# Decoder layer: pair 4 mixed alone, gate ahead of the factor, ScalarE and TensorE in the closing norm

## Chip, cores and metric

One core of one Trainium2 chip. The metric is the device time of one execution in microseconds; a kernel's time is the median of its runs. Engines: TensorE (PE), VectorE (DVE), ScalarE (ACT), GpSimd (POOL) and SyncE (SP, which here only issues transfers).

## What is computed

One decoder layer in float32 on x of 16 x 56 x 128, with post-norm after each of three blocks.

```python
def layernorm(x): return (x - mean(x)) / sqrt(var(x) + 1e-5)

# block 1: gated mixer
z = causal_conv4(x @ in_proj_w) + conv_b         # values, gate, scores
p_w = exp(clip(score_scale * s_raw)) * time_weight
re, im = cumsum(p_w * poly * cos(x_val * theta)) / den, cumsum(... sin ...) / den
rs = rsqrt(mean(re**2 + im**2) + 1e-5)           # the factor, per head
y = re * rs * norm_scale @ W_re + im * rs * norm_scale @ W_im
x = layernorm(x + (y * silu(gate)) @ out_proj_w)
# block 2: attention over a context of 1500 x 96
q, k, v = x @ Wq + bq, ctx @ Wk + bk, ctx @ Wv + bv
x = layernorm(x + softmax(q @ k.T / sqrt(128)) @ v)
# block 3: 8 experts, top 2 of them per token, then two norms
h = relu(x @ W1[e].T + b1[e]); o = h @ W2[e].T + b2[e]
x = layernorm(layernorm_gamma_beta(x + sum(router_w[e] * o)))
```

## The kernel before, in words

Each engine has its own hand-written list of instructions, in strict order, and meets the others through counting semaphores: an instruction that waits holds all that stand behind it on its engine. The 896 tokens are eight pairs of batch rows (112 tokens, 0 to 7), and for block 1 two halves of four pairs (c = 0, 1).

**Block 1** works with channels on partitions. For each half: projection and convolution (L490), angles, products, scans (L1242), group sums and squares (L500, L509). Then VectorE makes the variance (`variance`, L1281), ScalarE turns it into the factor (`factor`, L887 and L889), VectorE multiplies factor and gate and then y (`gated`, L1288 and L1291), TensorE projects out (`project_out`, L518), and VectorE adds x (`mixed`, L1297), takes the moments (`mixed_stats`, L1304, L1307) and, after ScalarE's reciprocal deviation (`mix_inv_std`), normalises (`mixed_norm`, L1313). `X1_PARTS` says which pairs are normalised, turned (`turn_x1`, L526; `x1T_copy`, L905) and made into queries (`query_keys`, L533; `queried_keys`, L917) together: pair 0, pairs 1 to 3, and pairs 4 to 7. `keep_warm` (L478) are matmuls on constants.

**Block 2** is a loop of seven turns and a last one. In turn i TensorE makes the scores of pair i+1 (L543), sums the context of pair i-1 (L566), turns the weights of pair i (L553, in three thirds), and finishes pair i-1 (`turn_sum`, `values`). VectorE takes the maximum (L1366) of pair i+1, copies turned weights (L1470) and makes the norm of pair i-1 (L1477 to L1489); ScalarE makes the exponential (L926). The second half of block 1 is woven into turns 0 to 2. Also woven in: the router (logits, top two, ranks, slots), the split of the expert weights into a high and a low float16 half (high on ScalarE, `split_high`, L991 and L993; low on POOL for experts 0 to 4, `split_low`, L1734; m_wh and m_wl count them in order of (weight, expert)), and of x2 into row halves (`high_rows`, L981; `low_rows`, L1725). POOL's list then goes on: after the low halves of (0,4) and (1,4) it makes the low rows of pair 4 and then scatters the rows of pairs 2 to 6 to the experts' slots in memory, two scatters a pair (L1750), with short pauses between.

**Block 3.** SP waits for all 14 scatters and loads the first tile of each expert (L453). TensorE runs the sequence: pair 7 with experts 0 to 4, 20 tiles of 128 rows (each turned, L744; hidden layer, L765 and L767; output, L784), pair 7 with experts 5 to 7. ScalarE weights a tile's output (L1097), and POOL scatters it to `ret` (L1832).

**Tail.** SP loads `ret` for pairs 0 to 6 in four parts (L464). TensorE adds both returned rows to x2 in PSUM (L806). q = 0 to 3 are two pairs each; pair 7 is summed in `acc` by VectorE and is in q = 3. On VectorE, `returned(q)` takes the moments (L1668, L1671), and `last_sum(q)` centres and multiplies by gamma (L1679), multiplies by the reciprocal deviation and adds x2 + beta (L1684), and takes the second moments (L1688, L1691). ScalarE makes the reciprocal deviations (`final_inv_std`, L893 and L895) and the last norm (`final_norm`, L1123), for which VectorE prepares the bias (`final_bias`, L1698). SP stores two pairs at a time (L468).

The functions, with their lines:

## Time and profile before

| | |
|---|---|
| median of 3 runs | 206.45 us (205.98 to 206.97) |
| the profiled execution, its own time | 205.7 us |
| its span | 203.9 us |
| busy: PE, DVE, ACT, POOL | 173.8, 154.4, 117.6, 61.7 us |
| granted TensorE clock, mean | 0.97 |

The span is what the profiler recorded, from the first to the last event; the 1.8 us beside it belong to the execution's own time. All times below count from the span's start. In a timeline row stand the start, the duration, engine, line, operation and operands, how many instructions were merged, and in brackets how long the engine was idle before and what released it. Starts of neighbouring instructions can lie closer than their durations, as they overlap by a few tens of ns.

### The profile page before, as it was taken

Reading aid. Unit: us, or ns where it says so; the run is one execution under the profiler, and the core shown is the slowest. Engines: PE = TensorE matmul, PEld = TensorE weight load, DVE = VectorE, ACT = ScalarE, POOL = GpSimd, SP = SyncE. Lnnn points to the kernel's source line nnn. Section 1 sums busy time; section 2 is a strip of 40 time slices with the busy share of each in tenths; the row PEclk is TensorE's granted clock in tenths of the full one; section 3 lists DMA queues with packets and bytes.
Section 4 is the critical chain, followed back from the end, with each engine's and each line's share of the span. In section 5 each row is a group of like instructions: output and inputs, shape, how many; then the busy total and the mean of one; then the engine's idle time right before and its main releaser. Section 6 shows DMA issues by size and latency. Waiting matters only on the chain.

```text
span 203.9 us, 4768 instructions
## 1 busy us (share of the span) xinstructions
PE 173.8 (85%) x1721; PEld 127.5 (63%) x1721; DVE 154.4 (76%) x394; ACT 117.6 (58%) x246; POOL 61.7 (30%) x82
## 2 busy tenths in 40 slices
PE   7999999969799978799799998785999999996400
PEld 6554556644353664564656787584999999994300
DVE  1659999988979668558967885677688888743890
ACT  2189979722664515697676954442566777650544
POOL 4000000000040000029697568881045655550000
PEclk9999999999999999999999999997899999999965
DMA  6999999993899278779856911104234100005011
GB/s 133 335 212 294 229 296 259 407 412 140 217 351 323 81 253 208 270 187 309 208 200 189 345 47 36 35 25 106 57 83 104 40 22 26 19 0 161 2 45 45
DMA packets 13467, 34.20 MB, mean 168 GB/s; under 512 B 2096, under 2 KB 5606, under 8 KB 13443
## 3 DMA queue, kind: packets, MB, share of 16 engines
q1 hardware_dynamic: 12356, 32.27, 53.0%
q0 software_dynamic: 1088, 1.62, 2.6%
q8 instruction: 14, 0.23, 0.5%
q14 instruction: 9, 0.07, 0.1%
HBM read 28.01 MB, written 6.38 MB: 169 GB/s over the span
## 4 chain that ended last, share of the span: by engine, by line
PE 53%; DVE 20%; issue 10%; POOL 8%; ACT 4%; DMA 2%; POOLq 0%; ACTq 0%; DVEq 0%; SPq 0%
PE bank L490 9%; POOL ret L1832 8%; PE bank L543 8%; PE bank L566 6%; PE bank L509 5%; PE bank L500 5%; PE bank L553 5%; PE bank L478 4%; DVE neg_max L1366 2%; PE bank L767 2%; PE bank L784 2%; DVE ph L1470 2%; DMA ctxT_slot<-ret 1%; DVE xtok L1684 1%; PE bank L806 1%
## 5 line engine op out<-in xcount | busy, mean ns | idle before, releaser
L1084 ACT ACTIVATE ctx_slot<-bank 128x512 f16<-128x512 f32 (+1 forms) x28 | 16.3, 582 | 18.8 <-PE bank L767 18.7
L1832 POOL DMA_INDIRECT ret<-ctx_slot,ctxT_slot x20 | 19.7, 986 | 24.5 <-ACT ctx_slot L1097 20.8
L1598 DVE SCALAR_TENSOR_TENSOR ctx_slot<-bank,ctx_slot 128x512 f16<-128x512 f32 (+1 forms) x28 | 18.8, 671 | 9.6 <-ACT ctx_slot L1084 7.2
L543 PE MATMUL bank<-ctxT_slot,w_conv 97*64 97x500 f32 x96 | 21.8, 589 | 2.4 <-ACT pc L926 1.4
L1754 POOL TENSOR_TENSOR home<-home 128x896 f32<-128x896 f32 x1 | 2.1, 2077 | 55.3 <-ACT home L882 55.3
L490 PE MATMUL bank<-xpad,w_conv 128*128 128x448 f32 x48 | 18.5, 544 | 0.0
L784 PE MATMUL bank<-home,ctx_slot 128*112 128x128 f16 (+1 forms) x192 | 14.7, 227 | 3.2 <-DVE ctx_slot L1598 3.2
L1366 DVE TENSOR_REDUCE neg_max<-bank 120x1 f32<-120x1500 f32 x8 | 13.7, 1714 | 4.5 <-PE bank L543 4.5
L1734 POOL TENSOR_TENSOR home<-w_raw,home 128x512 f16<-128x512 f32 x10 | 11.5, 1164 | 14.8 <-DVE neg_max L1366 14.8
L1242 DVE TENSOR_TENSOR_SCAN home<-reset,home 128x896 f32<-128x896 f32 x8 | 15.8, 2008 | 0.0
L566 PE MATMUL bank<-ctx_slot,ph 125*64 125x96 f32 x336 | 15.4, 248 | 0.0
L784 PEld LDWEIGHTS bank<-home,ctx_slot 128*112 128x112 f16 (+1 forms) x192 | 12.6, 121 | 3.7 <-DVE ctx_slot L1598 3.5
L490 PEld LDWEIGHTS bank<-xpad,w_conv 128*128 128x128 f32 x48 | 9.1, 193 | 9.2 <-issue 8.7
L1750 POOL DMA_INDIRECT slots<-mix,slot_i x14 | 13.5, 963 | 4.6 <-issue 3.7
L566 PEld LDWEIGHTS bank<-ctx_slot,ph 125*64 125x64 f32 x336 | 14.1, 133 | 1.2 <-issue 0.7
L478 PE MATMUL bank<-reset 128*128 128x224 f32 x48 | 13.4, 424 | 1.4 <-DVE reset L1145 1.4
L543 PEld LDWEIGHTS bank<-ctxT_slot,w_conv 97*64 97x64 f32 x96 | 6.2, 133 | 13.0 <-issue 10.9
L765 PE MATMUL bank<-half_sb,b_hl 128*128 128x112 f16 (+1 forms) x64 | 13.8, 221 | 0.3 <-DVE turned_late L1561 0.3
L500 PE MATMUL bank<-home,w_blk 128*128 128x448 f32 x32 | 12.9, 545 | 0.0
L478 PEld LDWEIGHTS bank<-reset 128*128 128x128 f32 x48 | 10.7, 235 | 2.9 <-DVE reset L1145 1.4
L893 ACT ACTIVATE lnv<-mv,cst 112x2 f32<-112x2 f32 (+3 forms) x11 | 3.2, 293 | 15.6 <-DVE mv L1307 6.3
L767 PE MATMUL bank<-ctx_slot 128*128 128x128 f16 x144 | 12.0, 219 | 0.0
(223 smaller groups left out, 433.5 us busy)
## 6 DMA issues: line engine op xcount, KB each, us to landing
ctx_slot<-ctx SPq DMA_DIRECT2D x16, 576.0 KB, 5.7
ctxT_slot<-ctx_T SPq DMA_DIRECT2D x16, 562.5 KB, 9.5
w_raw<-w SPq DMA_DIRECT2D x16, 256.0 KB, 6.9
slots<-w_raw SPq DMA_DIRECT2D x4, 910.0 KB, 26.1
ctxT_slot<-slots SPq DMA_DIRECT2D x20, 65.0 KB, 1.9
...
```

What stands on the lines that cost most here:

```text
L478: mm = pe.matmul(bank[:, to, 0:HW // 2], reset[:, 0:D], reset[:, 0:HW // 2], start=True, stop=True)
L490: mm = pe.matmul(bank[:, Z[c, g], 0:HW], w_conv[:, g, k, :], xpad[:, HB * c:HB * (c + 1), k:k + L], start=(k == 0), stop=(k == TAPS - 1))
L500: mm = pe.matmul(bank[:, Y_BANK[c], 0:HW], w_blk[:, j, :], terms[:, j * HW:(j + 1) * HW], start=(j == 0), stop=(j == 2 * M - 1))
L543: mm = pe.matmul(bank[j * GAP:j * GAP + rows, n, 0:SN], qk_all[:, at:at + rows], ctxT_slot[:, s, j, n * SN:(n + 1) * SN], start=True, stop ...
L566: mm = pe.matmul(bank[j * GAP:j * GAP + rows, SUM_BANKS[i], 0:DC], expT_sb[i][:, c, j * GAP:j * GAP + rows], ctx_slot[0:KP, s, j, c, :], s ...
L767: mm = pe.matmul(to, w[:, 0, part, at], x[:, half, 0:cols], start=False, stop=(m == 2))
L784: mm = pe.matmul(to, h_[:, n % 3, f, 0:cols], w[:, 1, part, f * D:(f + 1) * D], start=False, stop=(h_ is hl and f == FC - 1))
L1084: nc.scalar.activation(hh[:, n % 3, :, 0:cols], bank[:, n % 3, :].rearrange("p (f t) -> p f t", f=FC) [:, :, 0:cols], ACT.Relu).then_inc(t ...
L1242: return V.tensor_tensor_scan(sums[:, w], reset[:, 0:W2], terms[:, w], 0.0, ALU.mult, ALU.add)
L1366: V.tensor_reduce(neg_max[0:GT, :], bank[0:GT, 0:SB, 0:SN], AX.XY, ALU.max, negate=True).then_inc(a_max, 1)
L1598: V.scalar_tensor_tensor(hl[:, n % 3, :, 0:cols], bank[:, n % 3, :].rearrange("p (f t) -> p f t", f=FC) [:, :, 0:cols], 0.0, hh[:, n % 3, ...
L1832: G.indirect_dma_start(ret[:], bass.IndirectOffsetOnAxis(ap=xs_u[:, t, D + 1:D + 2], axis=0), out_st[:, t % OB, :], None, bounds_check=2 * ...
```

## The change

Block 1, second half: `X1_PARTS` has four parts, the third being pair 4 and the fourth pairs 5 to 7. Pair 4 is mixed, normalised in turn 1 and turned and queried in turn 2; pairs 5 to 7 are mixed in turn 1, have their moments and norm in turn 2 and are turned and queried in turn 3. y is multiplied by the gate before the factor is there, and by the factor afterwards (one multiply behind it, as before two); the projection of the second half moves ahead of the last third of the turned weights and its sum. In the front, the norm of pair 0 moves before the second half of the cosine products, and two of three `keep_warm` go. ScalarE's `split_high` are dealt out anew over the turns: 1, 2, 1, 3, 2 in turns 1 to 5 and one behind the loop (before: 1, 3, 2, 2, 2). POOL's list is the same.

Tail: pair 7 is done first and alone. For pairs 0 to 6 VectorE centres, ScalarE multiplies by the reciprocal deviation (`scaled`), TensorE adds that and x2 + beta in PSUM (`with_x2`), and VectorE takes the second moments there. The last norm is ScalarE's for q = 0 and 1, and VectorE's for pair 7, q = 2 and pair 6. There are five stores instead of four.

```diff
-X1_PARTS = (range(0, 1), range(1, PPH), range(PPH, PAIRS))
-T_BANK, QK_BANK = (4, 3, 7), (6, 5, 7)
+X1_PARTS = (range(0, 1), range(1, PPH), range(PPH, PPH + 1), range(PPH + 1, PAIRS))
+T_BANK, QK_BANK = (4, 3, 7, 7), (6, 5, 7, 7)
...
+SUM_AT, NORM_AT = (3, 7, 0, 1), (2, 5, 6, 4)
...
-    for q in range(4):
-        sp_.wait_ge(f_out, q + 1)
-        w = slice(2 * q, 2 * q + 2)
+    for n, w in enumerate((slice(XP, PAIRS), slice(0, 2), slice(2, 4), slice(4, 6), slice(6, XP))):
+        if n in (1, 2):
+            sp_.wait_ge(f_out, n)
+        else:
+            sp_.wait_ge(f_outv, n - 1 if n else 1)
         sp_.dma_start(out[:, w, :], x1[:, w, :]).then_inc(s_store, 16)
-    sp_.wait_ge(s_store, 16 * 4)
...
     def turn_x1(n):
         pe.wait_ge(s_x1, n + 1)
+        if n == 3:
+            pe.wait_ge(a_qksb, n)
...
-        pe.wait_ge(a_qksb, 1 if i == 0 else 2 if i < PPH else 3)
+        pe.wait_ge(a_qksb, 1 if i == 0 else 2 if i < PPH else 3 if i == PPH else 4)
...
     def logits(i):
         pe.wait_ge(a_x2T, i + 2)
+        if i == 0:
+            pe.wait_ge(a_qksb, 4)
...
         if i in (4, 6):
             ranks((4, 6).index(i))
+        if i in (2, 3):
+            turn_x1(i)
         if i:
             context_sum(i - 1)
         if i == 2:
-            turn_x1(2)
+            query_keys(2)
         turn_weights(i, 0)
         turn_weights(i, 1)
-        if i == 2:
-            query_keys(2)
+        if i == 1:
+            project_out(1)
+        if i == 3:
+            query_keys(3)
         if i:
             turn_sum(i - 1)
         turn_weights(i, 2)
         if i == 0:
             group_sums(1, 1)
-        if i == 1:
-            project_out(1)
         if i:
             values(i - 1)
...
-    keep_warm(3, 0)
+    keep_warm(1, 0)
...
+    def added(to, rows_, start=False, stop=False):
+        width = rows_.shape[1] * D
+        return pe.matmul(bank[0:PT, to, 0:width], ident[0:PT, 0:PT], rows_, start=start, stop=stop)
+
+    def returns(q):
+        w = slice(2 * q, min(2 * q + 2, XP))
+        added(SUM_AT[q], x2[:, w, :], start=True)
+        pe.wait_ge(g_ld[q], 16)
+        added(SUM_AT[q], got[:, w, 0, :])
+        added(SUM_AT[q], got[:, w, 1, :], stop=True).then_inc(f_y, 1)
+
+    def with_x2(q):
+        w = slice(2 * q, min(2 * q + 2, XP))
+        added(NORM_AT[q], x2b[:, w, :], start=True)
+        pe.wait_ge(f_scaled, q + 1)
+        added(NORM_AT[q], acc[:, w, :], stop=True).then_inc(f_sum, 1)
 
     pe.wait_ge(t_hl, len(SEQUENCE))
...
+    pe.wait_ge(t_acc, E)
+    pe.wait_ge(m_x2b, PAIRS)
+    returns(0)
+    returns(1)
+    returns(2)
+    with_x2(0)
+    returns(3)
+    with_x2(1)
+    with_x2(2)
+    with_x2(3)
...
     def attend_turn(i):
+        if i in (2, 3):
+            x1T_copy(i)
         if i + 1 < PAIRS:
             weights_exp(i + 1)
         if i == 1:
             factor(1)
         if i == 2:
-            x1T_copy(2)
+            queried_keys(2)
+            mix_inv_std(3)
         if i:
             turned_sum(i - 1)
+        if i == 1:
+            mix_inv_std(2)
+        if i == 3:
+            queried_keys(3)
         turned_copy(i)
         if i == 0:
             square(1, M, M + 2)
             square(1, M + 2, 2 * M)
-        if i == 2:
-            queried_keys(2)
         if i:
-            if i == 1:
-                mix_inv_std(2)
             attended_inv_std(i - 1)
         if i == 1:
             split_high(0, 0)
         if i == 2:
             split_high(1, 0)
             split_high(0, 1)
-            split_high(1, 1)
         if i == 3:
             high_rows(0)
         if i >= 3:
             high_rows(i - 2)
-        if 3 <= i < 6:
-            split_high(0, i - 1)
-            split_high(1, i - 1)
         if i in (3, 5):
             route_weights((3, 5).index(i))
+        if i == 3:
+            split_high(1, 1)
+        if i == 4:
+            split_high(0, 2)
+            split_high(1, 2)
+            split_high(0, 3)
+        if i == 5:
+            split_high(1, 3)
+            split_high(0, 4)
...
     high_rows(PAIRS - 3)
+    split_high(1, POOL_SPLITS - 1)
     turned_copy(PAIRS - 1)
...
+    def scaled(q):
+        act.wait_ge(f_cent, q + 1)
+        act.wait_ge(f_rstd, q + 2)
+        for j in range(2 * q, min(2 * q + 2, XP)):
+            ins = nc.scalar.activation(acc[:, j, :], acc[:, j, :], ACT.Copy, scale=rstd[:, j:j + 1])
+        ins.then_inc(f_scaled, 1)
...
+            ins = nc.scalar.activation(x1[:, j, :], bank[0:PT, NORM_AT[q], (j % 2) * D:(j % 2 + 1) * D],
+                                       ACT.Identity, bias=nmr[:, j:j + 1], scale=rstd2[:, j:j + 1])
         ins.then_inc(f_out, 1)
...
     final_inv_std(0, False)
+    final_inv_std(0, True)
     final_inv_std(1, False)
-    final_inv_std(0, True)
+    scaled(0)
     final_inv_std(2, False)
-    final_norm(0)
+    scaled(1)
     final_inv_std(1, True)
     final_inv_std(3, False)
+    scaled(2)
+    final_norm(0)
+    final_inv_std(2, True)
+    final_inv_std(4, False)
+    scaled(3)
     final_norm(1)
-    final_inv_std(2, True)
-    final_norm(2)
     final_inv_std(3, True)
-    final_norm(3)
+    final_inv_std(4, True)
...
+    def with_gate(c):
+
+        dve.wait_ge(s_gate, c + 1)
+        dve.wait_ge(s_ys, c + 1)
+        return own.mark(V.tensor_tensor(y_gated[:, c, :], y_gated[:, c, :], gate[:, c, :], ALU.mult))
+
+    def gated(c, multiplied):
+
+        own.need(multiplied)
         dve.wait_ge(s_f, c + 1)
-        dve.wait_ge(s_gate, c + 1)
-        a = own.mark(V.tensor_tensor(gate[:, c, :], gate[:, c, :], sc[:, c, :], ALU.mult))
...
     variance(0)
-    weights(1)
-    gated(0)
+    multiplied = with_gate(0)
+    weights(1, between=lambda: gated(0, multiplied))
     cos_terms(1, 0)
     dve.wait_ge(s_xtok, 16)
-    summed = mixed(0)
+    summed = mixed(0, range(PPH))
     mixed_stats(0, summed)
+    mixed_stats(1, summed, between=lambda: mixed_norm(0))
     cos_terms(1, 1)
-    mixed_norm(0)
-    mixed_stats(1, summed)
...
         maximum(i + 1)
         if i == 1:
             dens.append(denominator(1, scan_weights()))
             variance(1)
+            multiplied = with_gate(1)
+        inverse(i)
+        if i == 1:
+            gated(1, multiplied)
         if i == 2:
-            mixed_norm(2)
-        inverse(i)
+            mixed_stats(3, last_mixed)
         if i >= 2:
             x2T_copy(i - 2)
         if i in (4, 6):
             place((4, 6).index(i))
         if i:
             sum_copy(i - 1)
-        if i == 1:
-            gated(1)
         turned_copy(i)
+        if i == 2:
+            mixed_norm(3)
         if i == 0:
             scan_im(1, 0)
             scan_im(1, 1)
             scan_y(1)
         if i == 1:
-            mixed_stats(2, mixed(1))
+            mixed_stats(2, mixed(1, X1_PARTS[2]))
+            last_mixed = mixed(1, X1_PARTS[3])
+            mixed_norm(2)
...
+    def last_pair():
+
+        j = XP
+        dve.wait_ge(t_acc, E)
+        dve.wait_ge(m_x2b, PAIRS)
+        moments(0, lambda j: acc[:, j, :], f_var)
+        dve.wait_ge(f_var, 1)
+        a = own.mark(V.scalar_tensor_tensor(acc[:, j, :], acc[:, j, :], mv[:, j, 0:1], par("gamma", PT),
+                                            ALU.subtract, ALU.mult))
+        own.need(a)
+        dve.wait_ge(f_rstd, 1)
+        a = own.mark(V.scalar_tensor_tensor(acc[:, j, :], acc[:, j, :], rstd[:, j:j + 1], x2b[:, j, :],
+                                            ALU.mult, ALU.add))
+        own.need(a)
+        moments(0, lambda j: acc[:, j, :], f_var2)
...
+        moments(q + 1, returned_at, f_var)
+        dve.wait_ge(f_var, q + 2)
+        for j in range(2 * q, min(2 * q + 2, XP)):
+            ins = V.scalar_tensor_tensor(acc[:, j, :], returned_at(j), mv[:, j, 0:1], par("gamma", PT),
+                                         ALU.subtract, ALU.mult)
+        ins.then_inc(f_cent, 1)
+
+    def summed(q):
+        dve.wait_ge(f_sum, q + 1)
+        moments(q + 1, normed_at, f_var2)
...
+    def vector_final(n):
+
+        dve.wait_ge(f_rstd2, n + 1)
+        for j in range(XP, PAIRS) if n == 0 else range(2 * n - 2, min(2 * n, XP)):
+            ins = V.tensor_scalar(x1[:, j, :], normed_at(j) if n else acc[:, j, :], mv[:, j, 0:1],
+                                  rstd2[:, j:j + 1], ALU.subtract, ALU.mult)
+        ins.then_inc(f_outv, 1)
+
...
+    last_pair()
     returned(0)
+    vector_final(0)
     returned(1)
-    last_sum(0)
+    summed(0)
     returned(2)
     final_bias(0)
-    last_sum(1)
+    summed(1)
     returned(3)
     final_bias(1)
-    last_sum(2)
-    last_sum(3)
-    final_bias(2)
-    final_bias(3)
+    summed(2)
+    summed(3)
+    vector_final(3)
+    vector_final(4)
```

## Rows read from the trace of the kernel before

**Rows 1.** Busy time in two windows: PE, PEld, DVE, ACT, POOL, granted clock, DMA.

```profile
141.00:144.00 3.00, 3.00 (x34) 3.00 (x33) 1.62 (x4) 1.04 (x2) 0.00 (x0) 0.50 0.52 116
...
193.70:198.80 5.10, 0.00 (x0) 0.00 (x0) 4.86 (x23) 2.28 (x9) 0.00 (x0) 0.64 0.15 45
```

**Rows 2.** Timeline of VectorE, starts of the maximum: start, duration.

```profile
51.08 1.72 DVE L1366 TENSOR_REDUCE neg_max<-bank 120x1 f32<-120x1500 f32 x1 [0.54 <-PE bank L543]
...
65.39 1.69 DVE L1366 TENSOR_REDUCE neg_max<-bank 120x1 f32<-120x1500 f32 x1
...
79.22 1.71 DVE L1366 TENSOR_REDUCE neg_max<-bank 120x1 f32<-120x1500 f32 x1
...
88.79 1.72 DVE L1366 TENSOR_REDUCE neg_max<-bank 120x1 f32<-120x1500 f32 x1 [1.74 <-PE bank L543]
...
96.86 1.71 DVE L1366 TENSOR_REDUCE neg_max<-bank 120x1 f32<-120x1500 f32 x1
```

**Rows 3.** Timeline of VectorE, gate, mix and norm of turns 1 and 2.

```profile
72.07 0.61 DVE L1288 TENSOR_TENSOR mix<-mix 128x448 f32<-128x448 f32 x1
...
75.57 0.69 DVE L1297 TENSOR_TENSOR x<-bank,xtok 112x512 f32<-112x512 f32 x1 [1.10 <-PE bank L518]
...
80.85 1.11 DVE L1313 TENSOR_SCALAR x<-x,mv,rstd 112x128 f32<-112x128 f32 x4
```

**Rows 4.** Timeline of TensorE, turns 1 and 2.

```profile
75.68 2.73 PE L543 MATMUL bank<-ctxT_slot,w_conv 97*64 97x500 f32 x12
...
82.02 0.60 PE L526 MATMUL bank<-small_sb,x 112*128 112x112 f32 x4 [0.22 <-DVE x L1313]
...
83.34 0.92 PE L533 MATMUL bank<-xv,w_qk 128*97 128x448 f32 x2
```

**Rows 5.** Timeline of ScalarE, a weight split and the loop's end.

```profile
78.83 0.61 ACT L991 ACTIVATE w_raw<-w_raw 128x512 f32<-128x512 f32 x1
79.47 0.63 ACT L993 ACTIVATE home<-w_raw 128x512 f16<-128x512 f32 x1
...
120.27 0.40 ACT L981 ACTIVATE mix<-rows_late 112x256 f16<-112x256 f32 x1
122.04 0.56 ACT L931 COPY home<-bank 125x480 f32<-125x480 f32 x1 [1.37 <-PE bank L553]
```

**Rows 6.** Timeline of POOL, around the first scatter of group 1.

```profile
115.73 2.28 POOL L1734 TENSOR_TENSOR home<-w_raw,home 128x512 f16<-128x512 f32 x2
119.69 0.68 POOL L1725 TENSOR_TENSOR mix<-rows_late,mix 112x256 f16<-112x256 f32 x1 [1.68 <-ACT mix L981]
120.52 0.95 POOL L1750 DMA_INDIRECT slots<-mix,slot_i  x1 [0.15 <-POOL mix L1725]
...
136.16 0.95 POOL L1750 DMA_INDIRECT slots<-mix,slot_i  x1 [0.17 <-issue]
```

**Rows 7.** SP's queue, landing of its line 453, and TensorE at tile 0.

```profile
138.50 3.65 SPq L453 DMA_DIRECT2D ctxT_slot<-slots  x8
...
DMA to landing us min/median/max: 1.8/2.3/3.0
...
140.54 0.68 PE L784 MATMUL bank<-home,ctx_slot 128*112 128x128 f16 x4 [2.41 <-DVE ctx_slot L1598]
141.01 0.42 PE L744 MATMUL bank<-half_sb,ctxT_slot 128*128 128x128 f16 x2
```

**Rows 8.** Groups by shape, 186 to 204 us: busy us, mean ns, idle before.

```profile
L1123 ACT ACTIVATE x<-xtok,nmr,rstd 112x128 f32<-112x128 f32 x8 | 3.5, 481 | 1.7 <-DVE nmr L1698 1.7
L806 PE MATMUL bank<-ctxT_slot,small_sb 112*112 112x256 f32 x12 | 3.2, 387 | 1.7 <-DMA ctxT_slot<-ret 1.7
...
L1684 DVE SCALAR_TENSOR_TENSOR xtok<-xtok,rstd,rows_late 112x128 f32<-112x128 f32 x8 | 2.5, 349 | 0.1
L893 ACT ACTIVATE lnv<-mv,cst 112x2 f32<-112x2 f32 x8 | 2.3, 293 | 9.3 <-DVE mv L1671 6.1 <-DVE mv L1691 3.0
```

**Rows 9.** Timeline, the last instruction of ScalarE.

```profile
200.75 0.88 ACT L1123 ACTIVATE x<-xtok,nmr,rstd 112x128 f32<-112x128 f32 x2 [0.23 <-DVE nmr L1698]
```

88 lines of the change are left out of this document (32 added, 56 removed).

## The prediction

> **What bounds the kernel now.** I read the page's strip of 40 slices first: TensorE is at nine tenths or more almost everywhere and breaks off only near slice 27 and at the end. The chain that ended last then shows four stretches in which different things are late.
>
> First, the attention turns. The starts of the maximum on VectorE mark them [rows 2]. From turn 4 on one turn takes some 7.5 to 8.7 us, but turn 1 (65.39 to 79.22) takes 13.8 and turn 2 (79.22 to 88.79) takes 9.6. In these two turns the second half of the first block (squares, gate, output projection, four pairs mixed, normalised and turned at once) stands in the engines' queues ahead of the attention's next scores, which TensorE could start only at 75.68 [rows 4].
>
> Second, the scatters on POOL. From the first one of group 1 at 120.52 ten scatters run to 137.1 with only POOL's own work between them (low halves, weights, pauses) [rows 6]; the one that began at 136.16 releases the loads of the tiles at 138.50 [rows 7].
>
> Third, the experts. TensorE turns tile 0 at 141.01 [rows 7]; the load, issued at 138.50, landed by the shortest and the median time of its line at 140.3 to 140.8. VectorE's table of tiles let TensorE go at 140.54 [rows 7], so both paths end within about 0.5 us of each other. From there to 184 TensorE is full, and that stretch of 43 us has a fixed length.
>
> Fourth, the tail. Between 193.7 and 198.8 VectorE is busy 4.86 of 5.1 us, ScalarE 2.28, TensorE nothing [rows 1]. VectorE bounds it, until the last ScalarE norm, which starts at 200.75 [rows 9] and ends at 201.63; span 203.9.
>
> **Front (before turn 0).** The gate multiply moves ahead of the factor's arrival and only one multiply stays behind it, so y_gated is ready 0.6 us sooner (one of two multiplies; the second half's takes 0.61 [rows 3]). The projection, the first transpose and the first scores follow it on TensorE, and the first maximum, which waited 0.54 us for these scores [rows 2], then comes when VectorE is free. I take -0.5 (ends 0 and -0.65). Two fewer warming groups cost nothing: TensorE waits for VectorE there anyway.
>
> **Turn 1.** The factor is covered by the gate multiply; one multiply remains, and the projection stands before the last third of the turned weights instead of behind it. Second gate ready: 71.75 instead of 73.34 (0.5 of it from the front). The copies of the turned weights start 1.2 us earlier, the scores of turn 2 at 74.2 instead of 75.68. Behind them VectorE no longer does four pairs at once: one pair mixed (0.3, from the 0.69 of four [rows 3]), its statistics, then the add of the other three (0.55) while ScalarE finds the first deviation. Its path to the attended norm is now 3.6 us from 73.25, done at 76.85, as TensorE's scores end (74.2 + 2.73 [rows 4]). Maximum of turn 2 at 77.0 instead of 79.22 [rows 2]: -2.2 so far.
>
> **Turn 2.** On TensorE one transpose (0.2) and a query of one pair (0.25) replace four transposes of 0.60 together and a query of 0.92 [rows 4]. Before, the transposes waited for VectorE's four norms (1.11 at 80.85 [rows 3]); now the norm of pair 4 was done in turn 1, and statistics (1.0) and norm (0.85) of pairs 5 to 7 lie beside TensorE's 7.8 us of work. Next maximum at 84.8 instead of 88.79: -4.0.
>
> **Turn 3.** What was put off is paid here: three transposes (0.5), a query of three pairs (0.75), and a wait of some 0.1 us, as the logits use its bank and the next scores need its copy. Turn 3 was VectorE-bound by 0.5 us at its end, which covers part. Next maximum 93.8 instead of 96.86 [rows 2]: -3.1.
>
> **Turns 4 to 6.** ScalarE now splits three weight halves in turn 4 instead of two; a split is 0.61 + 0.63 [rows 5]. It had 0.4 us of idle time, so the exponential is 0.8 us late, of which 0.3 to 0.45 reach TensorE through the turned sum. Against it TensorE waited 0.8 us in turn 4 behind VectorE, part of which goes. I take **g = 3.1 us** as the gain at the end of the loop (ends 2.0 and 3.9: all of turn 3 and the late exponential uncovered; or turn 4's wait gone as well).
>
> **The wait this adds, on POOL.** POOL's list is unchanged: low half of (0,4), of (1,4), low rows of pair 4, first scatter of group 1. The high half of (1,4) used to be made in turn 5; POOL had both low halves by 118.01 and then waited 1.68 us for the rows [rows 6]. Now it comes after ScalarE's rows of pair 5, which end at 120.67, in the 1.37 us hole before the turned copy at 122.04 [rows 5]. In the old clock: high half at 121.85, low half at 123.1 (1.14 each, half of 2.28 [rows 6]), scatter at 123.9 instead of 120.52. That is 3.4 us later; the loop brings it forward by g. Net for the scatter chain: 3.4 - 3.1 = +0.3. Queued behind it on POOL are all ten scatters, which nothing else paces, and behind these SP's loads. The load of tile 0 lands at 140.6 to 141.1 against 141.0 for TensorE's turn before, so **the loop's gain of 3.1 is almost all lost: 0.0** (with g at its ends: +1.3 and -0.7). TensorE arrives at tile 0 three microseconds early and stands.
>
> That gap touches the clock. After the present gap TensorE's granted clock was 0.50 for 141 to 144 [rows 1], that is 1.2 GHz, and full again behind it. It will stop sooner and resume as late, so the slow stretch ends somewhat later: +0.2 (ends 0 and +0.5). The Trainium skill ("TensorE: Matmul & The Clock Gate", HAM oscillation) says the same of idle gaps; the trace agrees with its half rate.
>
> **Tail.** (a) Pair 7 is done from 184.75, while VectorE waits for the returns until 187.7; of its work moments, centring and scaling, 1.2 us, leave the busy stretch. (b) Seven scale-and-adds, 0.349 each and paced 0.31 [rows 8], leave VectorE: 2.2. (c) Pair 7's final norm enters, +0.34, and 0.2 for small gaps that two pairs shared. VectorE's work from 187.65 to its last moments is then 11.45 - 1.2 - 2.2 + 0.34 + 0.2 = 8.6 us, which would end at 196.3. (d) The hand-overs: centred -> ScalarE scale (0.87 a pair, as two of the 0.481 norms [rows 8]) -> TensorE add (0.387 a 256-wide matmul [rows 8], twice that at the lower clock) -> moments. Written out in order, VectorE waits 0.35 at the first sum, 0.5 at the second bias and 0.5 at the last sum, since ScalarE has 9.0 us of work from 188.5 in strict order: last moments at 197.7. (e) Deviation 0.53 (0.293 [rows 8] and 0.20), and one norm of 0.34 on VectorE: 199.2. Before, 2.5 us lay behind the last moments (two ScalarE norm pairs). With issue and landing as before the end moves from 203.9 to 201.7: **-2.2**. Ends: no waits, -3.6; every one of seven hand-overs costing 0.3 more, and the fifth output transfer queued behind the fourth, -0.5. I take the middle since the rows of each part are in the same stretch.
>
> By row, ScalarE's 112x128 pass costs 0.481 and VectorE's scale-and-add 0.349 [rows 8]. The Trainium skill ("ScalarE: Activation LUTs", Rules for kernel authors) says to use VectorE, not ScalarE, for add and mul. By that rule alone the sum would gain nothing at (b); I go by the window, where VectorE is full and ScalarE less than half.
>
> **Sum.** 0.0 + 0.2 - 2.2 = -2.0 on the profiled execution, whose time is 205.7: 203.7. It lay 0.75 below the median of 206.45; the median becomes 204.4.
>
> **Rivals.**
> 1. *The loop's gain reaches the tiles.* If the last low half is ready earlier than I count, or scatters can close up, tile 0 comes up to 2.5 us sooner: 204.4 - 2.5 = 201.9. For: the table of tiles and all TensorE work arrive early. Against: POOL's strict order and its solid row of scatters [rows 6].
> 2. *ScalarE becomes the tail's bound.* Its 9.0 us in strict order, with the 0.481 passes ahead of deviations that VectorE awaits, could swallow the 2.2: 206.2 to 206.6. It decides if ScalarE idles under 0.3 us from 188.5 on. The skill's rule above would have this outcome. Against: ScalarE's 2.28 of 5.1 [rows 1].
> 3. *Slower: the wait on the last high half outweighs all.* If turns 1 and 2 give nothing (the same VectorE work in pieces ends as late), the front's 0.5 stays and turn 3's 1.35 us and the exponential's 0.45 are paid: g = -1.3. The scatters then start 4.7 late, the load of tile 0 lands near 145.25, +4.25; with +0.2 and the tail's -2.2 the time is 208.7. It decides from g = -0.1 down (3.5 - 0.45 of slack + 0.2 - 2.2 is +1). Against: the 13.8 us of turn 1 are plainly queueing.
> 4. *Small gains*: g = 2 and a tail of -1.2 give +1.3 + 0.2 - 1.2: 206.7.
>
> **Chances.** Forecast, 203.2 to 205.4: 0.56. Rival 1: 0.17. Rivals 2 and 4, no change: 0.20. Rival 3: 0.07. A run of this kernel can tell about 0.5% (1 us) from no change. Faster 0.73, same 0.20, slower 0.07. The range takes in the forecast, most of rival 1 and the better part of 2 and 4: 202.2 to 206.2.
>
> **What would show it.** Right: maxima near 77, 84.8 and 93.8; an idle time of POOL ahead of its low half of (1,4), with the first group-1 scatter at 120.5 to 121.2; TensorE idle 3 us or more before the turn of tile 0, released by a DMA, near 141; VectorE's last norm near 199.3. Wrong: scatter (2,0) before 119 (rival 1) or after 123.5 (rival 3); ScalarE without idle time in the tail (rival 2).

## The result, and the profile after

| | before | after |
|---|---|---|
| median of 17 runs each, same chips | 205.93 us (205.09 to 207.30) | 203.24 us (201.37 to 205.70) |
| ratio, 95% interval | | 0.9845 (0.9813 to 0.9876) |
| the profiled execution, its span | 205.7, 203.9 us | 202.66, 200.9 us |
| busy: PE, DVE, ACT, POOL | 173.8, 154.4, 117.6, 61.7 us | 178.9, 154.1, 119.0, 61.5 us |

Three of the 17 executions after (204.50, 204.56 and 205.70) lie over 1.5% above the fastest of their kernel, and such executions are left out of every ratio and interval and of the medians in the table of the experiments; without them the median after is 202.87 us (201.37 to 204.15). The kernel is 1.55% faster, 3.1 us by these medians, 2.7 by those of the table above and 3.0 by the two profiled executions. The forecast was 204.4 us, 1.0% under the median it started from (206.45, of three runs; with 17 that median is 205.93). The direction holds and 203.24 lies in the range, but the gain is half as large again as forecast.

**Loop.** Timeline of VectorE after, the maximum at the start of turn 1 and the last one (start, duration), answering to [rows 2]:

```profile
64.50 1.69 DVE L1421 TENSOR_REDUCE neg_max<-bank 120x1 f32<-120x1500 f32 x1
...
108.71 1.71 DVE L1421 TENSOR_REDUCE neg_max<-bank 120x1 f32<-120x1500 f32 x1
```

Those between start at 76.39, 84.10, 92.56 and 100.05. Turn 1 shrank from 13.83 to 11.89 us and turn 2 from 9.57 to 7.71; turn 3 took 8.46 instead of 8.07. Against before the loop is 4.30 us ahead at 92.56, 5.56 ahead at 100.05 (105.61), and only 4.33 ahead at 108.71 (113.04). Two small VectorE operations say where it was lost again (same view):

```profile
106.39 2.09 DVE L1544 TENSOR_SCALAR rows_late<-res,attend_mv,attend_rstd 112x128 f32<-112x128 f32 x1
...
110.78 2.21 DVE L1471 TENSOR_TENSOR slot_c<-chosen,slot_e 112x32 f32<-112x32 f32 x1
...
116.51 0.35 DVE L1544 TENSOR_SCALAR rows_late<-res,attend_mv,attend_rstd 112x128 f32<-112x128 f32 x1
```

The norm L1544 takes 0.35 us at 116.51 and 2.09 at 106.39. The third row is also the norm of pair 5, the last thing that POOL's rows need from the loop; before it stood at 119.34, so the loop's gain there is g = 2.83. These starts are of one profile each, and the front moves between profiles: the first maximum stands at 50.20 after and 51.08 before, but at 50.40 in the kernel "tail only" below, which has the old front.

**POOL.** Timeline of POOL after, answering to [rows 6]:

```profile
111.78 1.16 POOL L1813 TENSOR_TENSOR home<-w_raw,home 128x512 f16<-128x512 f32 x1
119.09 1.15 POOL L1813 TENSOR_TENSOR home<-w_raw,home 128x512 f16<-128x512 f32 x1 [6.16 <-ACT home L1020]
120.20 0.68 POOL L1804 TENSOR_TENSOR mix<-rows_late,mix 112x256 f16<-112x256 f32 x1
121.04 0.94 POOL L1829 DMA_INDIRECT slots<-mix,slot_i  x1 [0.15 <-POOL mix L1804]
...
136.67 0.95 POOL L1829 DMA_INDIRECT slots<-mix,slot_i  x1 [0.17 <-issue]
```

POOL stands 6.16 us for the high half of (1,4), which ScalarE makes behind the loop (L1020 at 118.39). The first scatter of group 1 is at 121.04 against 120.52, although the loop is almost three microseconds early; the last begins at 136.67 instead of 136.16, and SP's loads at 139.07 instead of 138.50 [rows 7].

**TensorE at tile 0.** Timeline of TensorE after, answering to [rows 7], and the windows around it (columns as in [rows 1]):

```profile
139.60 0.43 PE L795 MATMUL bank<-home,ctx_slot 128*112 128x128 f16 x4 [2.42 <-DVE ctx_slot L1659]
140.87 0.33 PE L755 MATMUL bank<-half_sb,ctxT_slot 128*128 128x128 f16 x2 [0.84 <-DMA ctxT_slot<-slots]
```

```profile
126.00:130.00 4.00, 3.26 (x26) 2.59 (x27) 1.63 (x11) 1.95 (x8) 3.26 (x6) 0.67 0.11 32
130.00:134.00 4.00, 4.00 (x45) 3.96 (x45) 1.85 (x10) 1.67 (x5) 3.25 (x6) 0.50 0.11 30
134.00:138.00 4.00, 3.13 (x54) 2.85 (x52) 3.62 (x14) 2.12 (x4) 3.25 (x7) 0.98 0.11 31
138.00:141.00 3.00, 0.56 (x7) 0.42 (x7) 2.33 (x8) 0.00 (x0) 0.80 (x3) 1.00 0.25 64
141.00:144.00 3.00, 3.00 (x33) 3.00 (x32) 1.16 (x4) 1.06 (x2) 0.00 (x0) 0.50 0.45 97
```

The first two of these windows before:

```profile
126.00:130.00 4.00, 2.62 (x17) 1.78 (x18) 3.23 (x19) 1.68 (x7) 3.24 (x8) 1.00 0.10 29
130.00:134.00 4.00, 3.65 (x62) 3.29 (x63) 2.32 (x14) 2.03 (x6) 3.25 (x7) 1.00 0.12 33
```

The turn begins at 140.87 instead of 141.01, released by the load. TensorE stands 2.42 us for VectorE's table of tiles, as it did before (2.41 [rows 7]), and 0.84 us more for the load; only these 0.84 are new. So the loop's gain is lost in two places. One is the load, which comes no earlier because the scatters do not. The other is TensorE itself. It begins pair 7's hidden layer at 128.11 instead of 130.94, the whole 2.83 us early, but the granted clock is down to 0.50 for 130 to 134, where it was 1.00 before. Its last work ahead of the table ends at 137.18 instead of 138.13, and the table lets it go at 139.60 instead of 140.54: 0.94 us early.

**Tail.** The first returned part reaches TensorE at 186.44 (186.54 before); the span ends 14.46 us later instead of 17.36. Timeline after, the end of VectorE's and ScalarE's work, answering to [rows 9]:

```profile
197.00 0.29 ACT L920 ACTIVATE lnv<-mv,cst 112x2 f32<-112x2 f32 x1
197.31 0.18 DVE L1724 BATCH_NORM_AGGREGATE mv<-stat 112x2 f32<-112x6 f32 x1
197.32 0.20 ACT L922 ACTIVATE rstd<-lnv 112x2 f32<-112x2 f32 x1
197.52 0.29 ACT L920 ACTIVATE lnv<-mv,cst 112x1 f32<-112x1 f32 x1
197.56 1.05 DVE L1773 TENSOR_SCALAR x<-bank,mv,rstd 112x128 f32<-112x128 f32 x3
197.85 0.20 ACT L922 ACTIVATE rstd<-lnv 112x1 f32<-112x1 f32 x1
```

The last moments end at 197.49 (199.15 before), and the last deviation (197.52 to 198.05) is made while VectorE already normalises pairs 4 and 5. The window 193 to 198 reads:

```profile
193.00:198.00 5.00, 1.61 (x8) 0.90 (x6) 3.57 (x19) 4.38 (x17) 0.00 (x0) 1.00 0.09 26
```

VectorE, 4.86 of 5.1 us before [rows 1], has 1.4 us of idle time; ScalarE is now the fuller one at 4.38. VectorE's longer waits are these three, at the first sum, the second bias and the last sum:

```profile
191.32 0.49 DVE L1721 BATCH_NORM_STATS2 stat<-bank 112x6 f32<-112x128 f32 x2 [0.72 <-PE bank L816]
...
195.53 0.16 DVE L1767 SCALAR_TENSOR_TENSOR nmr<-mv,rstd 112x2 f32<-112x2 f32 x1 [0.59 <-ACT rstd L922]
...
196.97 0.30 DVE L1721 BATCH_NORM_STATS2 stat<-bank 112x6 f32<-112x128 f32 x1 [0.60 <-PE bank L816]
```

None of this is what one would see if VectorE's work alone set the new end.

### The profile page after: what moved, and what is told of

It reads as the page before. It is cut to its first block, busy times and chain, and to the rows that moved or that the text cites. A ratio compares the mean times of both kernels' runs of the same rounds, so it can differ in the third digit from the quotient of the medians.

```text
span 200.9 us, 4804 instructions
## 1 busy us (share of the span) xinstructions
PE 178.9 (89%) x1735; PEld 131.3 (65%) x1735; DVE 154.1 (77%) x390; ACT 119.0 (59%) x257; POOL 61.5 (31%) x82
## 3 DMA queue, kind: packets, MB, share of 16 engines
q0 software_dynamic: 1088, 1.62, 2.6%
## 4 chain that ended last, share of the span: by engine, by line
PE 25%; POOL 21%; issue 17%; ACT 5%; DVE 5%; DMA 4%; POOLq 1%; DVEq 0%; ACTq 0%; SPq 0%
POOL ret L1911 9%; PE bank L550 5%; POOL slots L1829 5%; PE bank L573 3%; PE bank L560 3%; PE bank L816 2%; POOL home L1813 2%; PE bank L505 2%; PE bank L514 2%; POOL mix L1804 2%; PE bank L778 2%; DMA ctxT_slot<-ret 1%; PE bank L795 1%; DMA slots<-mix,slot_i 1%; DMA ret<-ctx_slot,ctxT_slot 1%
## 5 line engine op out<-in xcount | busy, mean ns | idle before, releaser
L1813 POOL TENSOR_TENSOR home<-w_raw,home 128x512 f16<-128x512 f32 x10 | 11.5, 1161 | 24.8 <-DVE neg_max L1421 12.9
L795 PE MATMUL bank<-home,ctx_slot 128*112 128x128 f16 (+1 forms) x192 | 15.2, 232 | 2.5 <-DVE ctx_slot L1659 2.4
L573 PE MATMUL bank<-ctx_slot,ph 125*64 125x96 f32 (+1 forms) x336 | 15.4, 248 | 0.0
L795 PEld LDWEIGHTS bank<-home,ctx_slot 128*112 128x112 f16 (+1 forms) x192 | 13.1, 125 | 2.9 <-DVE ctx_slot L1659 2.8
L573 PEld LDWEIGHTS bank<-ctx_slot,ph 125*64 125x64 f32 (+1 forms) x336 | 14.0, 133 | 1.2 <-issue 0.7
L776 PE MATMUL bank<-half_sb,b_hl 128*128 128x112 f16 (+1 forms) x64 | 14.8, 234 | 0.1
L483 PE MATMUL bank<-reset 128*128 128x224 f32 x44 | 11.7, 405 | 1.4 <-DVE reset L1193 1.4
L483 PEld LDWEIGHTS bank<-reset 128*128 128x128 f32 x44 | 9.3, 223 | 2.8 <-DVE reset L1193 1.4
L514 PE MATMUL bank<-home,small_sb 128*128 128x448 f32 x28 | 11.0, 545 | 0.0
```

What stands on the lines that cost most here:

```text
L483: mm = pe.matmul(bank[:, to, 0:HW // 2], reset[:, 0:D], reset[:, 0:HW // 2], start=True, stop=True)
L573: mm = pe.matmul(bank[j * GAP:j * GAP + rows, SUM_BANKS[i], 0:DC], expT_sb[i][:, c, j * GAP:j * GAP + rows], ctx_slot[0:KP, s, j, c, :], s ...
L795: mm = pe.matmul(to, h_[:, n % 3, f, 0:cols], w[:, 1, part, f * D:(f + 1) * D], start=False, stop=(h_ is hl and f == FC - 1))
```

## The experiments

Theory A is the prediction's: the loop's gain ends in POOL's list, and the tail gains because VectorE's work there shrinks. Three groups of kernels ran, each on one chip with its own runs of the kernel before. In the text below, "tail" is the time from the first returned part at TensorE to the span's end.

| kernel | median (runs in it, of all) | ratio to before, same chip | tail |
|---|---|---|---|
| loop only | 205.93 (12 of 12) | 0.9976 (0.9943 to 1.0009) | 17.74 |
| tail only | 202.60 (6 of 6) | 0.9820 (0.9777 to 0.9864) | 14.52 |
| scatter first | 201.39 (6 of 6) | 0.9771 (0.9724 to 0.9818) | 14.59 |
| TensorE kept warm | 203.15 (5 of 6) | 0.9845 (0.9789 to 0.9900) | 14.28 |
| scale on VectorE | 202.86 (6 of 6) | 0.9819 (0.9763 to 0.9875) | 14.33 |
| scale and add on VectorE | 202.66 (5 of 6) | 0.9794 (0.9743 to 0.9846) | 14.27 |
| bias split later | 203.04 (6 of 6) | 0.9842 (0.9797 to 0.9887) | 14.58 |
| scatter first and warm | 202.69 (4 of 6) | 0.9808 (0.9741 to 0.9874) | 15.93 |
| pair 7 first, ScalarE's last norm | 209.65 (5 of 6) | 0.9884 (0.9825 to 0.9942) | 15.50 |
| VectorE's last norm only | 208.10 (4 of 6) | 0.9860 (0.9809 to 0.9911) | 16.14 |
| scatter first, bias split later | 205.26 (6 of 7) | 0.9695 (0.9659 to 0.9731) | 14.26 |

The last three ran on a chip on which the kernel before takes 211.40 us; on the chips of the others it takes 206.24 and 206.65. The ratios are each to that chip's own runs of before. The new tail as it is in the change was profiled six times besides the changed kernel's own: 14.26 to 14.59 us in five of them, 15.93 in one (scatter first and warm). The old one took 17.36 and 17.74. So a difference of less than some 0.4 us between two tails says nothing.

### Each half of the change alone

Loop only: the changed kernel with the old tail.

```diff
-            last_pair()
             returned(0)
-            vector_final(0)
             returned(1)
-            summed(0)
+            last_sum(0)
...
-            vector_final(3)
-            vector_final(4)
+            final_bias(2)
+            final_bias(3)
```

> The changed kernel with the closing norm of the kernel before: front, loop and the splits' new places alone. Theory A (the forecast's: the loop's gain is lost in POOL's wait for the last high half): same time as the kernel before within 0.5 us; maximum of the last turn near 108.7 to 109, first scatter of group 1 near 121, first store of a weighted tile's scatter (POOL's first scatter to ret) near 149.2. Rival B (half or more of the loop's 2.8 us reaches the end): 204.5 or less where the kernel before has 205.9.

Tail only: the kernel before with the new tail (the same lines the other way round).

> The kernel before with the new closing norm alone. Theory A: the whole gain, 2.7 to 3.2 us below the kernel before, and from the landing of the first returned part to the end of the span 14.5 us against 17.4. Rival B: 1.5 us or less, the rest coming from the loop.

The loop alone gives nothing that can be measured (0.9976, the interval holds 1 and allows at most 1.2 us), the tail alone the whole gain (0.982). So the prediction's 0.0 for the loop is right within that interval. The marks that the text above names for the loop came 1.1 to 1.5 us late: last maximum at 110.14, first scatter of group 1 at 122.46, first return to memory at 150.52. The profiled execution is the slowest of the twelve, and its first turn is long; why, the section on the spread shows.

### The wait on POOL taken away

```diff
-            split_low(1, 4)
             low_rows(4)
             scatter(2, 0)
             plus_beta(4)
             scatter(2, 1)
+            split_low(1, 4)
```

> The changed kernel; POOL makes the low rows of pair 4 and both scatters of pair 2 before its low half of (1,4), whose high half comes late; nothing else differs. Theory A: the first scatter of group 1 moves from 121.0 to about 117.8, the scatters behind it gain 2 us, the load of tile 0 lands near 138.8, and TensorE's turn of tile 0 comes at 140.0 instead of 140.87, as VectorE's table of tiles lets TensorE go only at 139.6: 0.8 to 0.9 us below the changed kernel. Rival C (POOL's wait does not set the tiles' start): no change, within 0.3 us.

Timeline of POOL in this kernel:

```profile
117.13 0.67 POOL L1804 TENSOR_TENSOR mix<-rows_late,mix 112x256 f16<-112x256 f32 x1 [4.31 <-ACT mix L1008]
117.96 0.95 POOL L1829 DMA_INDIRECT slots<-mix,slot_i  x1 [0.15 <-POOL mix L1804]
...
119.50 0.95 POOL L1829 DMA_INDIRECT slots<-mix,slot_i  x1 [0.17 <-issue]
120.47 1.17 POOL L1813 TENSOR_TENSOR home<-w_raw,home 128x512 f16<-128x512 f32 x1
```

The scatter comes 3.08 us earlier, the last one begins at 134.68 instead of 136.67, and the tail starts at 184.81 instead of 186.44. By the ratios the kernel is 0.7% (1.5 us) under the changed one, whose interval (0.9813 to 0.9876) it just touches, and 0.5% under the tail alone, where the intervals overlap widely. But the scatters' two microseconds do not arrive as such. TensorE's timeline:

```profile
137.41 0.43 PE L795 MATMUL bank<-home,ctx_slot 128*112 128x128 f16 x4 [0.40 <-DVE ctx_slot L1659]
...
140.49 0.43 PE L795 MATMUL bank<-home,ctx_slot 128*112 128x128 f16 x4 [1.36 <-DVE ctx_slot L1659]
140.76 0.28 PE L755 MATMUL bank<-half_sb,ctxT_slot 128*128 128x128 f16 x2
```

The turn of tile 0 (L755) is at 140.76, no earlier than in the changed kernel (140.87), and no longer released by the load: TensorE had done its pair-7 work at half clock until shortly before, and that work is now the late one. The text above had the turn at 140.0, and there it went wrong. The 1.6 us by which this profile's tail starts earlier come behind the turn, with the clock, as the next section shows. So removing the wait takes the load off the path, and TensorE's own list takes its place.

### TensorE kept busy before tile 0

The rival to A here: the clock at half rate, not the load, sets the start of the tiles.

```diff
-                keep_warm(1, 4)
+                keep_warm(2, 4)
...
+                keep_warm(1, 4)
...
+                    if n == 2 and h_ is hl:
+                        pe.wait_ge(r_lg, PAIRS)
+                        pe.wait_ge(r_rk, len(GROUPS))
+                        keep_warm(6, 7)
```

> The changed kernel with more matmuls on constants in TensorE's gaps: two more in the last turn of the attention and six ahead of the last four matmuls of the third output (2.4 us of idle time while VectorE makes the table of tiles). Theory D (the half clock of 127 to 134 and of 141 to 144 costs time): the granted clock stays at 1.00 through 126 to 148, hidden and output layers in 141 to 144 take 1.5 us less, and TensorE's turn of tile 0 stays at 140.9, since a load releases it: 1.2 to 1.5 us below the changed kernel, and less spread between its runs. Rival E: the constants delay the router's transposes by more than the clock gives; same or slower.

The clock is 1.00 from 126 to 141 here, and nothing is gained (ratio 0.9845, as the changed kernel's): TensorE stands for the same load, and behind the stand the clock falls to 0.50 for 141 to 144. Its timeline:

```profile
137.60 0.39 PE L800 MATMUL bank<-home,ctx_slot 128*112 128x128 f16 x4
140.55 0.28 PE L756 MATMUL bank<-half_sb,ctxT_slot 128*128 128x128 f16 x2 [2.57 <-DMA ctxT_slot<-slots]
```

Both edits together, scatter first and warm:

> The changed kernel with POOL's scatters ahead of the low half of (1,4) and with the added matmuls on constants. With the load of tile 0 out of the way the clock should count now. Theory A with D: TensorE at full clock from 126 on, reaches tile 0 by 138.5, load landed at 138.8, POOL's first scatter to ret at 146.5 or earlier against 147.50 with the scatters alone: 0.5 to 1.5 us below that kernel. Rival J: VectorE's table of tiles bounds the start all the same; within 0.4 us of it.

Here the load is early and TensorE is ready for it:

```profile
138.27 0.43 PE L800 MATMUL bank<-home,ctx_slot 128*112 128x128 f16 x4
139.14 0.28 PE L756 MATMUL bank<-half_sb,ctxT_slot 128*128 128x128 f16 x2 [0.43 <-DMA ctxT_slot<-slots]
```

The profiles side by side, with the granted clock of two windows, the start of tile 0's turn, and the time from it to POOL's first return to memory:

| profile | clock 134-138; 141-144 | turn of tile 0 | to first return |
|---|---|---|---|
| before | 1.00; 0.50 | 141.01 | 8.16 |
| changed | 0.98; 0.50 | 140.87 | 8.38 |
| TensorE kept warm | 1.00; 0.50 | 140.55 | 8.38 |
| loop only | 0.84; 0.69 | 142.18 | 8.34 |
| scale on VectorE | 0.83; 0.70 | 141.30 | 8.37 |
| VectorE's last norm only | 0.79; 1.00 | 140.33 | 6.75 |
| scatter first, bias split later | 0.77; 1.00 | 141.73 | 6.74 |
| bias split later | 0.58; 1.00 | 141.24 | 6.76 |
| pair 7 first, ScalarE's last norm | 0.54; 1.00 | 142.34 | 6.75 |
| tail only | 0.50; 1.00 | 142.80 | 6.74 |
| scale and add on VectorE | 0.50; 1.00 | 142.60 | 6.76 |
| scatter first | 0.69; 1.00 | 140.76 | 6.74 |
| scatter first and warm | 1.00; 1.00 | 139.14 | 6.76 |

Half clock behind the turn costs 1.6 us. It is there in the five rows where 134 to 138 had a clock of 0.83 or more and TensorE then stood over 2 us, and absent in the eight others: seven ran at half clock for a larger part of that window (0.50 to 0.79), and in the last TensorE stood only 0.43 us. Only the last row has both, an early turn and a full clock, and its first return at 145.90 is 3.35 us ahead of the changed kernel's: 1.73 from the earlier turn, which neither edit gave alone, and 1.62 from the clock.

Its ratio is nevertheless 0.9808, no better than the changed kernel's within the intervals, so the times do not confirm what the profile gains. In the profile 3.57 us pass between the start of POOL's last return and SP's load, and the tail takes 15.93, its first part running at a granted clock of 0.59 (184 to 187). In the kernel kept warm that first interval is 2.97; in the eleven profiles without the added matmuls it is 2.18 to 2.20. So the matmuls that keep TensorE warm come with a loss at the other end, and both experiments with them show less than the clock alone would give. Why, no run shows.

### The tail taken apart

First the part that the prediction held to be the gain. Scale on VectorE: the multiplication by the reciprocal deviation goes back to VectorE as an operation of its own, and TensorE still adds. Scale and add on VectorE: both go back, as seven operations of 0.35 us, with pair 7 first and VectorE's last norm kept. The diff is that of the second.

```diff
-            with_x2(0)
...
-            scaled(0)
...
+            def summed(q, centred):
+                own.need(centred)
+                dve.wait_ge(f_rstd, q + 2)
+                for j in range(2 * q, min(2 * q + 2, XP)):
+                    b = own.mark(V.scalar_tensor_tensor(acc[:, j, :], acc[:, j, :], rstd[:, j:j + 1], x2b[:, j, :],
+                                                        ALU.mult, ALU.add))
+                own.need(b)
                 moments(q + 1, normed_at, f_var2)
```

> The changed kernel with the multiplication by the first reciprocal deviation back on VectorE, as a multiply of its own, seven of 112x128; TensorE still adds x2 + beta. Theory A (VectorE is the full engine of the tail): its seven passes of 0.28 to 0.35 us come on top, less the waits for ScalarE that go: 0.8 to 2.0 us above the changed kernel. Rival F (ScalarE's queue and the hand-over bound the new tail, so that VectorE is the better place): same or faster.

> The changed kernel with neither ScalarE's scale nor TensorE's add: VectorE scales and adds in one pass as in the kernel before and takes the moments from SBUF; pair 7 is still done first and VectorE still makes the closing norm of pairs 4 to 6. Theory A: seven passes paced 0.31 us (2.2) return, less about 0.9 us of waits for the two engines: 1.0 to 2.0 us above the changed kernel, so that 1.2 to 2.2 us of the tail's 3 remain with pair 7 and the last norm. Rival G (the gain is only in the order and the last norm): within 0.4 us of the changed kernel.

Neither costs anything: tails of 14.33 and 14.27 against 14.46, ratios of 0.9819 and 0.9794 against 0.9845. Theory A, at least 0.8 us slower, fell; rival F held, and G by the tails. The windows of the two tails, first the changed kernel's, then that of the kernel with both on VectorE, the second 1 us longer and with the wait in front of the first moments:

```profile
187.60:197.60 10.00, 6.99 (x34) 5.01 (x32) 7.61 (x39) 7.10 (x26) 0.00 (x0) 1.00 0.10 29
```

```profile
187.00:198.00 11.00, 4.25 (x22) 3.28 (x21) 9.52 (x47) 5.54 (x20) 0.00 (x0) 0.92 0.21 66
```

Cut exactly at the first and the last moments, the stretch is 9.89 us with 7.57 of VectorE and 6.99 of ScalarE in the changed kernel, and 9.99 with 9.43 and 5.04 in the other. VectorE works 1.9 us more and ScalarE 2.0 less, and the length is the same. What left VectorE came back as waits for the hand-overs: VectorE stands 2.3 us instead of 0.6. So something else in the tail gains; two parts are left, pair 7 in front and the last norm on VectorE. Each was left alone, on the changed kernel's loop. In the first, the norms of pairs 4 to 6 go back to ScalarE:

```diff
-            vector_final(3)
-            vector_final(4)
+            final_bias(2)
+            final_bias(3)
...
             final_inv_std(3, True)
+            final_norm(2)
             final_inv_std(4, True)
+            final_norm(3)
```

> The loop is the changed kernel's; in the tail ScalarE's scaling and TensorE's adding are gone (VectorE scales and adds) and ScalarE normalises pairs 0 to 6, as before; of the change's tail only this is left: pair 7 is finished on its own in front of the six others, and each pair is centred right behind its moments. From the first returned part at TensorE to the span's end: 17.74 us with the old tail on this loop, 14.27 with pair 7 first and VectorE's last norm. If pair 7's place is what gained (theory H): at most 15.0 us, kernel at most 203.4 us. If the last norm on VectorE is what gained (theory I): at least 17.0 us, kernel 205 to 206 us. If it is half and half, 15.5 to 16.3.

In the second, the old tail has only its last two `final_bias` and `final_norm` replaced (the diff is to the old tail; ScalarE's two norms go with it):

```diff
-            final_bias(2)
-            final_bias(3)
+            vector_final(2)
+            vector_final(3)
```

> The loop is the changed kernel's, the tail is the old one but for one thing: the last norms (pairs 4 to 7) are one VectorE operation each in place of VectorE's bias and ScalarE's pass. Theory H (pair 7's place gained): 17.0 us or more from the first returned part to the end, kernel 205.3 to 206.3 us. Theory I (the last norm gained): at most 15.0 us, kernel at most 203.4 us. The two runs should add up to the 3.3 to 3.5 us between the old tail and the new on this loop.

Both theories fell in their pure form: 15.50 and 16.14 us, the first inside the "half and half" of its text. The tail's two sections sort it out, each read from the last BATCH_NORM_AGGREGATE of VectorE in the timeline:

| tail | returned part to last moments | last moments to the end |
|---|---|---|
| before; loop only | 12.61; 12.91 | 4.75; 4.83 |
| VectorE's last norm only | 12.60 | 3.54 |
| pair 7 first only | 11.38 | 4.12 |
| scale and add on VectorE (both) | 11.14 | 3.13 |
| changed | 11.05 | 3.41 |

Pair 7 first takes 1.2 to 1.5 us from the first section (12.61 - 11.38 and 12.60 - 11.14) and 0.4 to 0.7 from the second (3.54 - 3.13, 4.83 - 4.12), where the last group is then one pair instead of two; the last norm on VectorE takes 1.0 to 1.3 from the second (4.12 - 3.13, 4.83 - 3.54). Together they are the 3.5 us from 17.74 to 14.27.

"Pair 7 first" stands for two edits that no run separates: in that tail VectorE also centres each pair right behind its moments. The windows give an estimate of the shares. From the first moments to the last, VectorE before has 10.38 us of work in 11.45, and with scale and add on it 9.43 in 9.99. So 0.95 is work that left the stretch and 0.5 idle time that is gone, and before 0.52 of idle time stood ahead of the second moments, where pair 7's norm and the first centring now stand.

The timelines of the ends say how the last norm works. Pair 7 first only:

```profile
203.50 0.18 DVE L1718 BATCH_NORM_AGGREGATE mv<-stat 112x2 f32<-112x6 f32 x1
203.60 0.13 DVE L1766 SCALAR_TENSOR_TENSOR nmr<-mv,rstd 112x2 f32<-112x2 f32 x1
203.76 0.88 ACT L1163 ACTIVATE x<-xtok,nmr,rstd 112x128 f32<-112x128 f32 x2 [0.29 <-DVE nmr L1766]
204.55 0.28 ACT L916 ACTIVATE lnv<-mv,cst 112x1 f32<-112x1 f32 x1
204.86 0.20 ACT L918 ACTIVATE rstd<-lnv 112x1 f32<-112x1 f32 x1
205.09 0.16 DVE L1766 SCALAR_TENSOR_TENSOR nmr<-mv,rstd 112x1 f32<-112x1 f32 x1 [1.36 <-ACT rstd L918]
205.29 0.49 ACT L1163 ACTIVATE x<-xtok,nmr,rstd 112x128 f32<-112x128 f32 x1 [0.23 <-DVE nmr L1766]
```

The last deviation waits behind ScalarE's norm of pairs 4 and 5, and then goes ScalarE, VectorE, ScalarE. In the changed kernel it is made beside VectorE's norm, and one operation without a bias follows.

### The spread of the runs

The changed kernel's 14 runs spread over 2.8 us, those of before over 2.2. The profile of the loop-only kernel has a first turn of 9.51 us instead of 7.65 and shows one cause (its timelines of ScalarE, VectorE and POOL):

```profile
57.16 0.31 ACT L970 ACTIVATE xpad<-xpad 40x128 f32<-40x128 f32 x1 [3.11 <-DMA xpad<-bias]
```

```profile
59.74 5.78 DVE L1262 TENSOR_TENSOR_SCAN home<-reset,home 128x896 f32<-128x896 f32 x2
```

```profile
59.85 3.78 POOL L1785 TENSOR_TENSOR home<-home 128x896 f32<-128x896 f32 x1 [56.74 <-ACT home L891]
```

In the changed kernel's profile these two take 3.93 and 2.08 us and are not at the same time. A bias load that lands late holds ScalarE, its squares come late, and POOL's fold falls onto VectorE's scans. Five profiles rank in this way: the scans take 3.93 without an overlap, 4.39 with 0.6 us of it (the load 1.51 late), 5.78 to 5.83 in three with 2.1 to 3.9 (the load some 3 late). One of these three is the kernel with the new tail only, so the late load is not of the change's making. In the three SP issued the load at 33.4 to 34.0 us, in the changed kernel's profile at 30.4. So ScalarE's squares were put ahead of the part that needs the load:

```diff
-            bias_high()
             square(1, 0, M)
+            bias_high()
```

> The changed kernel; ScalarE reads the expert biases behind the squares of turn 0 instead of in front. In one profiled run the bias transfer landed 3 us late, ScalarE's squares and with them POOL's fold slid onto VectorE's scans, and both took twice as long (5.78 against 3.93 us, 3.78 against 2.08). Theory H (this landing makes the spread between runs): no run with the scans at 5.8 us, lowest time unchanged, median 0.5 to 1.0 us below the changed kernel. Rival I: no change of median or spread, as the scatter chain hides it.

The spread is 1.9 us over its six runs, the ratio (0.9842) no better, so theory H's gain did not come. The spread shows nothing either: the tail alone, with the load in its old place, has 1.7 us over six. In the profile ScalarE reaches the part behind the load at 57.71 without a wait, and the scans take 3.93 us. With the scatter first as well:

> The changed kernel with two moves: POOL's scatter of tile 2's rows and the next ahead of the low halves of (1,4), and ScalarE's squares ahead of the part that waits for the bias load. Theory A: the loop's gain of 2.8 us goes through POOL's queue, last scatter 134.7 us or earlier, kernel 201.0 to 202.0 us with a narrower spread than 200.35 to 202.75, since no run then has the late first turn. Rival: the late first turn has nothing to do with the bias load: spread as wide as without (2.4 us), median within 0.4 of 201.4.

0.9695 on that chip, the best ratio of all. Five of its seven runs lie between 205.00 and 205.37, but the other two are 207.76 and 210.82, so the narrower spread is not shown. The changed kernel itself did not run on that chip, so its distance from this version is not measured directly; of the two halves of the new tail there, the better one is 2.8 us slower, of which the tails explain 1.9. Its profiled execution, 207.76, was not one of the five, so the rows of it say little about them.

So the late load is one cause that the profiles show, worth 1.9 us in the first turn, and how much of the spread it makes is open. The clock behind tile 0, worth 1.6 us, may be another: it differs between profiles of different kernels, but no kernel was profiled both with it and without.

## Why the prediction was right and wrong

**What bounds the kernel: read too smoothly.** The strip of before has TensorE at seven or eight tenths in eight of the slices from the 11th to the 27th, and at five in the 28th. No term of the sum rests on this.

**Front and turns 1 to 3: right in kind, too small.** The first maximum came at 50.20, 0.88 us early for a forecast of 0.5; as the old front has it at 50.40 in another profile, how much of this is the change's is open. Turn 2's maximum came at 76.39 for 77.0, turn 3's at 84.10 for 84.8, the next at 92.56 for 93.8.

**g: right by luck of two errors.** 2.83 us at the last norm, forecast 3.1. The loop was 5.56 us ahead at 100.05 and lost 2.7 again, most of it in the two VectorE operations of 2.09 and 2.21 us above. The step on turns 4 to 6 had ScalarE's exponential as the loss and no stall of VectorE beside POOL. The trace of before had a small one: the same norm takes 1.16 us instead of 0.35 at 95.33 (last section).

**POOL's wait: right; TensorE's clock ahead of tile 0: missed.** The first scatter of group 1 came at 121.04; the forecast was 123.9 - 3.1 plus 0.2 to 0.4, inside "120.5 to 121.2". The idle time ahead of the low half, the release by a DMA and the turn at 140.87 came as written, and the loop alone gives 0.9976. Rivals 1 and 3 fell with it. But TensorE did not arrive three microseconds early: it was 0.94 early at 139.60, and of its 3.3 us without work 2.4 had been there before. The half clock of 130 to 134, which the forecast does not have, had taken 1.9 of the 2.83 us, so even with an early load the turn would have come at 139.9 at best (139.60 and the 0.27 that four matmuls take there), and with the scatters first it came at 140.76. That the loop came out at nothing is therefore right, and the one reason given for it is half of it. The clock's +0.2 behind the turn fits (the turn 0.14 early, the first return 0.08 late), but I had not seen that the half clock there costs 1.6 us in all, or that a run may escape it.

**Tail: the step that failed.** Forecast 2.2, measured 2.9. Up to the last moments the sum was right by luck, for two terms were wrong against each other: (a) to (d) made -1.51, measured were -1.56. (b) less (d), 2.2 less 1.35, was to give 0.85 and gives 0.1 at most: the work that leaves VectorE is 1.86 us (9.43 - 7.57), and the waits that come for it are 1.76. The three waits stand where (d) had them, 0.72, 0.59 and 0.60 instead of 0.35, 0.5 and 0.5. And pair 7, (a) less (c), was to give 0.66 and gives 1.2 to 1.5: 0.95 of work, and some 0.5 of a wait before that the sum has no term for.

The term that makes the result's miss is (e): behind the last moments I forecast 4.0 us to the end, 0.75 less than before; it is 3.41, 1.34 less. The sum in (e) does not add up. Its two terms, 0.53 and 0.34, make 0.87, but it goes on 1.5, from 197.7 to 199.2; and from there to 201.7 it has 2.5 where "as before" is 2.27 (201.63 to 203.9). So 0.86 us of the 4.0 stand behind no term. Measured, the three norms on VectorE run in one row behind the last moments, the last deviation hides behind the first two of them, and they end after 1.12 us (197.49 to 198.61), with 2.29 to the end. That makes 0.6 of the missing 0.7 us.

What misled me in (b) was to take the work off a full VectorE [rows 1] at its full price. VectorE was the limit of the old tail, and taking pair 7's work off it did pay. But the scaling and adding that were handed on did not only leave VectorE: they put ScalarE and TensorE between VectorE's centring and its next moments, and the new waits were as long as the work.

**Rival 2 and the rule behind it.** Rival 2 fell: ScalarE has 2.1 us of idle time between 188.5 and 197.5, not under 0.3, and the tail gained 2.9. Rival 4, with g = 2 and a tail of -1.2, fell with 2.83 and -2.9. ScalarE's scaling took 0.40 us an operation and 0.69 a pair, not the 0.481 and 0.87 of [rows 8]; VectorE's takes 0.35. The rule of the Trainium skill ("ScalarE: Activation LUTs", Rules for kernel authors) that add and mul belong on VectorE would have left (b) without a gain. The trace agrees with it as far as that: moving them gained nothing. It lost nothing either.
